# A Perceiver kernel on one core: the sixteen 256-column matmuls of a tile placed singly between the 512-column ones

## The reference, cut to what matters

```
k = heads(key, Wk, bk);  v = heads(value, Wv, bv)      # 12544 x 512, 16 heads of 32
k_prime = relu(einsum('bhnd,fd->bhnf', k, Wkf)) * attention_mask[:, None, :, None]   # 64 features a head
kv = einsum('bhnf,bhne->bhfe', k_prime, v)             # summed over the 12544 rows
k_sum = sum(k_prime, axis=2)
```

## Time and profile before

| | |
|---|---|
| time, median of 3 runs | 862.82 us (862.41 to 862.89) |
| span of the profiled execution | 860.8 us |
| PE / PEld busy | 851.4 us (99%) / 731.0 us (85%) |
| DVE / ACT / POOL busy | 683.3 (79%) / 554.7 (64%) / 370.6 us (43%) |
| granted TensorE clock, mean over the span | 1.000 |

### The profile page before, as it was taken

The page is one execution under the profiler, slowest core; times in us unless marked ns, Lnnn a source line. Parts: engine busy times, 40 slices in busy tenths (PEclk is TensorE's granted clock), DMA queues, the critical chain, the costliest instruction groups (busy, mean ns, idle before and its releaser), DMA issues.

```text
span 860.8 us, 14422 instructions
## 1 busy us (share of the span) xinstructions
PE 851.4 (99%) x4618; PEld 731.0 (85%) x4618; DVE 683.3 (79%) x1075; ACT 554.7 (64%) x1009; POOL 370.6 (43%) x215
## 2 busy tenths in 40 slices
PE   8999999999999999999999999999999999999998
PEld 7888888888888888888888888888888889878767
DVE  5777777777777777777777777888888878779897
ACT  5666666666666666666666666666777656676563
POOL 2555454544555554445445555544454433220000
DMA  7212214010101010010101010101101000679740
GB/s 271 98 51 76 73 52 167 24 49 24 49 24 49 24 49 25 30 43 24 49 24 49 24 49 24 48 25 28 46 24 49 26 1 11 239 282 410 308 147 13
DMA packets 19529, 66.25 MB, mean 77 GB/s; under 512 B 2224, under 2 KB 2992, under 8 KB 19120
## 3 DMA queue, kind: packets, MB, share of 16 engines
q1 hardware_dynamic: 19072, 64.88, 20.9%
q10 hardware_dynamic: 432, 1.05, 0.3%
HBM read 65.66 MB, written 0.26 MB: 77 GB/s over the span
## 4 chain that ended last, share of the span: by engine, by line
PE 91%; issue 4%; DVE 2%; DMA 1%; POOL 1%; ACT 0%; POOLq 0%; ACTq 0%; SPq 0%; DVEq 0%
PE kv_ps L879 11%; PE f_ps L866 11%; PE v_bank L784 10%; PE v_bank L785 10%; PE v_bank L786 10%; PE k_bank L784 10%; PE k_bank L785 10%; PE k_bank L786 10%; PE kv_ps L1178 2%; PE kv_ps L1160 1%; DMA early<-in_wk 1%; PE f_ps L949 0%; PE f_ps L1050 0%; PE v_bank L968 0%; DMA ctx_raw<-in_ctx 0%
## 5 line engine op out<-in xcount | busy, mean ns | idle before, releaser
L461 POOL TENSOR_TENSOR ksum_acc<-ksum_acc,kf 128x1024 f32<-128x1024 f32 x97 | 233.0, 2402 | 86.7 <-DVE kf L1284 86.7
L454 POOL TENSOR_TENSOR ctx_lo<-ctx_raw,ctx_hi 128x512 fp32r<-128x512 f32 x92 | 119.7, 1301 | 274.0 <-ACT ctx_hi L532 274.0
L540 ACT ACTIVATE keys<-k_bank,bias_cols 64x512 fp32r<-64x512 f32 (+1 forms) x194 | 131.5, 678 | 148.6 <-PE k_bank L786 146.2
L1260 DVE SCALAR_TENSOR_TENSOR keys<-k_bank,bias_cols,keys 64x512 fp32r<-64x512 f32 (+1 forms) x194 | 143.2, 738 | 83.7 <-ACT keys L540 80.4
L1277 DVE TENSOR_TENSOR kf<-f_ps,fb 128x256 f32<-128x256 f32 x392 | 148.6, 420 | 16.8 <-ACT fb L557 5.6
L784 PE MATMUL v_bank<-wv_hi,ctx_lo 128*128 128x512 f32 x388 | 152.3, 392 | 0.0
L785 PE MATMUL v_bank<-wv_lo,ctx_hi 128*128 128x512 f32 x388 | 152.1, 392 | 0.0
L784 PE MATMUL k_bank<-ctx_hi,wk_lo 128*128 128x512 f32 (+1 forms) x392 | 151.4, 386 | 0.0
L785 PE MATMUL k_bank<-ctx_lo,wk_hi 128*128 128x512 f32 (+1 forms) x392 | 151.1, 385 | 0.0
L786 PE MATMUL v_bank<-wv_hi,ctx_hi 128*128 128x512 f32 x388 | 151.0, 389 | 0.0
L786 PE MATMUL k_bank<-ctx_hi,wk_hi 128*128 128x512 f32 (+1 forms) x392 | 149.9, 383 | 0.0
(11 more groups left out here) (245 smaller groups left out, 979.0 us busy)
## 6 DMA issues: line engine op xcount, KB each, us to landing
ctx_raw<-in_ctx SPq DMA_DIRECT2D x46, 512.0 KB, 3.3
early<-in_stream SPq DMA_DIRECT2D x15, 1024.0 KB, 8.4
raw<-in_stream SPq DMA_DIRECT2D x12, 1024.0 KB, 8.7
early<-in_stream SPq DMA_DIRECT2D x8, 512.0 KB, 4.2
early<-in_ctx SPq DMA_DIRECT2D x2, 512.0 KB, 6.1
early<-in_wv SPq DMA_DIRECT2D x1, 1024.0 KB, 7.8
early<-in_wq SPq DMA_DIRECT2D x1, 1024.0 KB, 9.2
early<-in_wo SPq DMA_DIRECT2D x1, 1024.0 KB, 7.1
```

Of the source, the lines that this page charges most:

```text
L454: pool.tensor_tensor(ctx_lo[:, s, :, cols], raw[:, :, t % 2 * P:(t % 2 + 1) * P], ctx_hi[:, s, :, cols].bitcast(f32), ALU.subtract).then_i ...
L461: pool.tensor_tensor(ksum_acc[:, :].rearrange("p (j f) -> p j f", f=P), ksum_acc[:, :].rearrange("p (j f) -> p j f", f=P), kf[:, t % 2, :, ...
L540: act.activation(keys_2[rows, s, 2 * m + h, 0:n], src[rows, 0:n], ACT.Identity, bias=bias_cols[rows, KC + m:KC + m + 1]).then_inc(k_hi_rea ...
L1260: dve.scalar_tensor_tensor(out=keys_2[other, s, 2 * m + h, 0:n], in0=src[rows, 0:n], scalar=bias_cols[rows, KC + m:KC + m + 1], in1=keys_2 ...
```

## The change

Only the order of TensorE's instructions in `period` changes. The number, the shape and the operands of the matmuls stay. The 4 matmuls of feature jobs 0 and 1 no longer stand ahead of the values but singly behind each of the first 4 of the 12 matmuls of the values. The 4 of jobs 2 and 3 stand singly behind the first 4 of the 12 of the keys, and the 8 of the features and values of the tile before stand singly behind the other 8. So the two waits of `key_values` now stand behind the fifth matmul of the keys, and the last matmul of the keys, which signals `k_done`, is now followed by one matmul of 256 columns and not by eight. The three products of a step (low*high, high*low, high*high) keep their order. `period_0` and `period_last` are unchanged, and so are all other engines.

```diff
--- before.py
+++ after.py
@@ -904,13 +904,59 @@
                     if t > 0:
                         key_values(t - 1, t + 1, first=t == 1)
 
+            def feature(c, s, n, t, j):
+
+                i = j // 2
+                if j % 2 == 0:
+                    if t == 0:
+
+                        pe.wait_ge(k_lo_ready, 2 * (KC * c + i + 1))
+
+                    pe.wait_ge(fsum_ready, JOBS * n + i - 1)
+                last = pe.matmul(f_ps[i % 2][:, (j % 2) * 2 * P:(j % 2 + 1) * 2 * P],
+                                 keys_2[:, s, j, t * P:(t + 1) * P], bd[:, :, :].rearrange("p x f -> p (x f)"),
+                                 start=True, stop=True)
+                if j % 2 == 1:
+                    last.then_inc(f_done, 1)
+
+            def one_of_three(out_ps, st_hi, st_lo, mv_hi, mv_lo, x, k):
+
+                return pe.matmul(out_ps, st_hi if x else st_lo, mv_lo if x == 1 else mv_hi,
+                                 start=k == 0 and x == 0, stop=k == KC - 1 and x == 2)
+
             def period(c, s, n_keys=CHUNK):
                 n = TILES * c
                 for t in range(TILES):
-                    jobs = [(c, s, n + t, t, i) for i in range(JOBS)]
-                    values(n + t, s, t, jobs[0:2])
-                    keys(c + 1, 1 - s, t, jobs[2:4], n_keys)
-                    key_values(n + t - 1, t + 1)
+
+                    pe.wait_ge(v_lo_ready, n + t)
+                    for k in range(KC):
+                        cols = slice(t * P, (t + 1) * P)
+                        for x in range(3):
+                            last = one_of_three(v_bank[:, :], ctx_hi[:, s, k, cols], ctx_lo[:, s, k, cols],
+                                                wv_hi[:, k, :], wv_lo[:, k, :], x, k)
+                            if k == KC - 1 and x == 2:
+                                last.then_inc(v_done, 1)
+                            if 3 * k + x < NPAIR // 2:
+                                feature(c, s, n + t, t, 3 * k + x)
+
+                    pe.wait_ge(ctx_lo_ready, TILES * c + n_keys // P)
+
+                    pe.wait_ge(k_lo_ready, 2 * (KC * (c + 1) + t))
+                    for k in range(KC):
+                        for x in range(3):
+                            last = one_of_three(k_bank[:, 0:n_keys], wk_hi[:, t, k, :], wk_lo[:, t, k, :],
+                                                ctx_hi[:, 1 - s, k, 0:n_keys], ctx_lo[:, 1 - s, k, 0:n_keys], x, k)
+                            if k == KC - 1 and x == 2:
+                                last.then_inc(k_done, 1)
+                            j = 3 * k + x
+                            if j < NPAIR // 2:
+                                feature(c, s, n + t, t, NPAIR // 2 + j)
+                            else:
+                                if j == NPAIR // 2:
+                                    pe.wait_ge(v_lo_ready, n + t)
+                                    pe.wait_ge(kf_lo_ready, n + t)
+                                last = key_value(j - NPAIR // 2, t + 1, False, False)
+                    last.then_inc(kv_done, 1)
 
             def period_last(c, s):
                 n = TILES * c
```

## The result

The changed kernel takes 877.38 us (median of 4 runs, 877.22 to 877.6) where the kernel before took 862.76 in the same comparison: 14.6 us more, ratio 1.017 with a 95% interval of 1.0155 to 1.0184. The profiled execution has a span of 875.2 us against 860.8, at the same granted clock of 1.000. Forecast were 873.1 us, slower, and a range of 865 to 880. The 871 to 875 that the forecast gave its own sum (with 42%) are missed.

A forecast was written before the change was run, and what follows sets the result against it. TensorE's instruction order was taken to set the time. Steady tiles 1.0, row sums 2.8, weight pieces 5.0, last period 1.0 and exit 0.5 sum to 10.3 us, on 862.8 making 873.1 us; range 865 to 880.

The forecast's parts named there:

- 68 steady tiles: Tiles without row sum or weight piece: each 7.41 us, 0.014 longer than before, 1.0 us in all.
- 8 tiles with a row sum: Tiles whose chain through ScalarE and VectorE takes 4.89 us: loop 7.75 us, 0.35 more each, 2.8 us.
- 12 tiles with a weight piece: Tiles whose chain through ScalarE and VectorE takes 4.96 us: loop 7.82 us, 0.42 more each, 5.0 us.
- last period: Four tiles with keys of 256 columns: first 0.43 us late, the other three 0.2 each, together 1.0 us.
- exit into `period_last`: Last keys read some 0.95 us later, ScalarE's first read-outs behind: between 0 and 0.95 us, estimate 0.5.
- Part 2, the new wait: Later `k_done` delays `kf_lo_ready`: steady tiles clear by 0.19 us, 20 tiles wait, loops of 7.75 and 7.82 us.
- Part 1, the rate: TensorE's alternating large and small matmuls: 0.350 us a pair, 7.41 us a tile, 0.014 longer than before.
- 3-and-2 turns: Stretch of `period_last` where 3 large and 2 small matmuls alternate: 0.927 us each against 0.907, 0.010 lost per small one.
- pure column rate: Rival, 12%: TensorE's alternation hides all loss at small matmuls, 68 x -0.147 = -9.9 us; total 861.0 us.
- Only the 0.12: Rival, 18%: each small TensorE matmul costs its 0.12 us and nothing else, pair 0.347; total 869.0 us.
- Every large one as slow as the worst: Rival, 18%: large TensorE matmuls behind small ones at the worst 0.235 us, pair 0.355; total 879.1 us.
- The wait does not bind: Rival, 10%: read-outs or VectorE come earlier than the chain says, only 88 x 0.014 = 1.2 us remain; total 864.0 us.

The follow-up runs named there:

- e3: Changed kernel with TensorE's order untouched; row sums and weight pieces moved to where ScalarE and VectorE wait for the keys: 871.42 us, ratio 1.0103.
- e1: Changed kernel, but the eight matmuls of features and values grouped again behind the keys; only feature jobs stand singly: 866.32 us, ratio 1.0043.
- e2: As e1, but each of the eight feature matmuls stands behind the first of a group of three large ones: 879.13 us, ratio 1.0194.
- e4: Changed kernel, but the eight matmuls of features and values stand in pairs behind the last four of the keys: 868.27 us, ratio 1.0064.
- e7: As e5, but feature jobs 0 and 1 stand behind the first large matmul of the values: 866.12 us, ratio 1.0037.
- e6: Kernel before, but four of the eight matmuls of features and values moved ahead, behind the eighth matmul of the keys: 863.71 us, ratio 1.0015.
- e5: Kernel before, but feature jobs 2 and 3 directly ahead of the features and values, one group of 16 small matmuls: 869.68 us, ratio 1.0083.
- e8: As e7, but row sums and weight pieces moved into idle time of ScalarE and VectorE: 861.6 us, ratio 0.9984.

## Why the prediction was right, and where it was off

The terms, forecast and measured (tile lengths of the two traces, times the count):

| term | forecast | measured |
|---|---|---|
| 68 steady tiles | 68 x 0.014 = 1.0 | 68 x 0.080, less 0.1 in the first few = 5.3 |
| 8 tiles with a row sum | 2.8 | 62.04 - 8 x 7.40 = 2.8 |
| 12 tiles with a weight piece | 5.0 | 93.64 - 12 x 7.40 = 4.8 |
| last period | 1.0 | 25.56 - 4 x 6.10 = 1.2 |
| exit into `period_last` | 0.5 | 0.5 |
| entry into the loop | not counted | -0.3 |
| sum | 10.3 | 14.4 before rounding (the span: 875.2 - 860.8) |

**Part 2, the new wait, held.** The later `k_done`, the 4.95 us through the other engines, the 0.14 to release, and the loop that feeds itself gave 7.82 and 7.75 us; measured were 7.80 and 7.755 on average. Term by term, for the weight piece: 0.43, 4.95, 0.14, 0.19 and six pairs in 2.09 (623.74 to 625.83), where 2.10 was forecast. e3 takes the extras out of the loop and e1 takes TensorE's part of it away; either removes the wait. The steady tile did not wait. The sign to look for was named less well: idle time of 0.3 to 0.5 us ahead of L879, released by VectorE. It shows as 0.23 on the load's row, labelled "issue", and as 0.37 at L916. The pages of ScalarE and VectorE alone would not have told: both are idle a quarter to a third of the time, and yet 20 tiles hang on them.

**Part 1, the rate, was mis-sized.** The forecast set its own test, that it was wrong on the rate if the steady tile departed from 7.41 by more than 0.04, and by this test it was: the tile is 7.48. That is the whole miss of the total: 5.3 us in the table and not 1.0, while the other terms together are 0.2 less than forecast. The direction did not hang on it, for 8.8 of the 10.3 us were the new waits and the last period. Two terms of the rate were off. A pair cost 0.3525 and not 0.350 (16 x 0.0025 = 0.04). And the 8 large ones alone I had put at the pure rate, though the kernel before already showed that large ones behind small ones are slowed; that is the other 0.03. The 3-and-2 turns gave 0.010 for each small one, near what a pair lost (0.3525 - 0.340 = 0.0125), but they say nothing of large ones that follow alone. The pure column rate, which would have made the change a gain, did not occur.

**What the rate depends on.** Read from the starts of the matmuls in the kernel before, a small one inside a group costs 0.0067 us over the column rate, and the return to large ones costs 0.027 once, spread over the next five. Cut short by the next small one it costs less, 0.006 behind one large one, and a single small one 0.003 (the numbers of e2's expectation). This rule gave 7.46 for e2 (measured 7.467), 7.45 for e4 (7.433), 7.386 for e7 (7.380) and 7.415 for e6 (7.407). It finds on which side of 7.400 each one lies and most of the distance. A fixed cost per small matmul puts e1 and e2 at the same length and e6 and e7 at 7.400, and all of that is refuted.

The rule does not give the alternation itself. The 7.44 expected of e1 was not made with it. With it, the changed kernel would have 15 returns cut short after one large one, a whole one and 16 singles, 15 x 0.006 + 0.027 + 16 x 0.003 = 0.165 over 7.253, or 7.42 us (measured 7.480), and e1 comes to about 7.42 too (7.440). In the steady alternation the large ones take 0.232, 0.240 and 0.236 in turn, on average 0.236 and not the 0.233 of the rule, and behind a wait of TensorE most take 0.230 in the same order. So the rate depends on what went before as well as on the order. Nor is the number of returns enough: e4 has 12 of them and is shorter than e1 and e2 with 9. What is shown is that alternation of all 16 is the longest of the steady tiles read, and that those with two groups are the shortest (7.400 and 7.380). What happens inside the engine at a return was not found; that stays open.

The weight load of a matmul starts with the matmul before it in the changed kernel as well (both rows at 618.38 above: the load for L916 and the matmul ahead of it): the cover was not widened by alternation, as the forecast had argued from the earlier trace rows.

**The rivals.** "Only the 0.12" (0.347 a pair) and the pure column rate fell with the 0.3525 of the steady tiles, though 0.347 is what the pairs behind a wait take. "Every large one as slow as the worst" had 0.355 a pair and 7.49 us a tile. The pair of 0.3525 lies midway between it and the forecast, the tile of 7.48 nearer to it, and its 879.1 us is closer to 877.4 than my 873.1: it deserved more than its 18%. Its reason held too: in the steady alternation the large ones take 0.236 on average, just over the worst row of before, and the small ones 0.117. The forecast's 68 x -0.147 for the pure column rate is -10.0 and not -9.9, which changes nothing. "The wait does not bind" fell.

## What to carry to other kernels

When work is moved on the engine that sets the time, follow each signal that it gives earlier or later through the fixed queues of the other engines back to the next instruction that needs it, and write that way as a loop: its length against the engine's own time says whether it binds, and tells it even for the few tiles in which something extra lies on the way. A slack measured in steady tiles says nothing of those. The other engines can slow each other in such a loop, as in e2 and e7, so durations are to be read again after a move. And small matmuls between large ones are not free fill: here alternation lost more at the large ones (0.009 each) than a small one saved against one in a group (0.003). Few groups were best for the rate, but the fewest (one, in e5) brought a wait that cost more than it could win.

## What the runs showed of the hardware that I had not expected

- A return from matmuls of 256 columns to those of 512 slows the next ones, which take 0.234, 0.236, 0.228, 0.232, 0.231 us and only then 0.227; in the kernel before it is the same within 0.001 whether 4 or 12 small ones went before. Alternating, the spacing settles into a cycle of three pairs of 1.06 us, 0.353 a pair, but runs at 0.347 a pair behind a wait.
- VectorE and GpSimd hold each other up: in e7 L1302 took 2.29 us beside GpSimd's L454 and 1.22 alone, L1364 1.45 beside L461, where the same work took 0.69 alone; in e8 L1367 took 1.37 beside L454. GpSimd's L454 ran from 613.77 to 615.06 and 1.22 more would end at 616.28; L1302 ended at 616.14. It goes by which starts first: L1302, started 0.01 ahead of L454 at 606.38, took 1.21, and then L454 took 2.36 and not 1.29. The Trainium skill (SBUF — State Buffer, section on the two separate sides) says that the two engines share a pair of ports, which a VectorE instruction with two inputs in SBUF and a GpSimd instruction that reads SBUF both want; the one that starts first holds it for its whole length, and the other blocks. The trace agrees, for L1302 starts 0.08 behind L454 and lasts about as if it had begun at its end.
